# Position bias added to the scores from three bf16 parts, adapters in pairs, and q and k spread in four pieces, in a four-layer transformer kernel

## The chip, the cores and the metric

The kernel runs as one program on one core of a Trainium2 chip. The metric is the device time in microseconds (us) of one execution. The kernel before was timed in three runs; its median is 2657.45 us, between 2647.17 and 2663.92.

## The reference, cut to what matters

x holds rows of D = 128; the kernel works on them in 8 batches of T = 512. Every layer does the same: `xn = layernorm(x)`, then `x = x + attention(xn) + feed_forward(xn)`.

```python
# layers 0 and 2: 16 heads of 8, causal; layer 2 masks with w*mask - (1-mask)*1e6
p = softmax(scores - max); oc = einsum('bhqk,bhkd->bhqd', p, v); return oc @ Wo.T + bo
# layer 0 ffn: 16 experts, top 4 by logits; layer 1 ffn: 8 experts, top 1
# layer 1 attention: 8 heads of 64, linear attention with a decay
S = g4 * S + einsum('bhi,bhj->bhij', kt, vt); z = g3 * z + kt      # q, k = elu + 1
y = num / den * gate
# layer 2 ffn: 8 autoencoders with 32 hidden; the best one's adapter is added
h = relu(einsum('btd,edh->ebth', x, Wd1) + bd1); recon = einsum('ebth,ehd->ebtd', h, Wd2) + bd2
idx = argmin(mean((recon - x) ** 2)); return base + adapter[idx](x)
# layer 3 attention: full, with a position bias of each head
rel = clip(pos[:, None] - pos[None, :] + (N - 1), 0, bias_table.shape[0] - 1)
energy = energy + bias_table[rel].transpose(2, 0, 1)
att = softmax(energy / (sqrt(C) * clip(temperature[0], 0.1, 10.0)))
# layer 3 ffn: top 2 experts chosen by the first token, mean of both
```

## The kernel before, in words

The four layers follow each other; within a layer all work is cut into 8 batches of 512 tokens. Layer 0 and layer 1 end with a routed stretch (the experts, some 485 to 795 us and 1245 to 1385 us of the span). A program of its own for each engine (PE is TensorE, DVE is VectorE, ACT is ScalarE, POOL is GpSimd, SP issues most DMAs) takes steps in the order of one list. `lay_out` (L774) makes it: each step has a time written by hand, in slots, and the list is sorted by it. A step carries the name of what it does; `own(n)` of each layer gives the steps of batch n that aren't attention. So moving a number moves the step past all others on its engine. An engine that waits in one step holds up all that stand behind it.

**Attention, layers 0, 2 and 3.** The 16 heads go in 4 groups of 4 (`HG`, `NG`). q and k are split into three bf16 parts, stored to DRAM (L494, L497) and read back spread over the partitions, so that one matmul of 72 rows (`KROWS`) gives the float32 product. `sp_expand` (L487) does this on SP: two halves of 8 heads, each one DMA for K (L516) and one for Q (L518); each load has a semaphore. The dictionary `behind_row` says which half waits until how many of the previous batch's rows of maxima are in: `{1: 3}` in layers 0 and 2 (half 1 waits for three rows), `{0: 2}` in layer 3 (half 0 waits for two). For each group: `pe_max` (L541, with the mask L547) makes the scores in rows of q, DVE reduces them to maxima (L558, in layer 3 also L564 with the tilted bias `L.tilt`), TensorE turns the maxima (L590), ACT copies them (L597), and `store_max_rows` (L524) sends them with a 12 KB DMA from ACT's queue into the last rows of Q, so that the next product already has the maximum taken off. Then `pe_scores` (L611) makes the scores in columns of k, ACT takes the exponential (L633), TensorE multiplies with v (L648), and the result is turned and divided (L656, L662, L668, L669). The first score of a group waits for that group's stored row. Layers 0 and 2 have 10 score slots a group, 40 a batch; layer 3 has 16, 64 a batch. The turned attention goes through L677 (TensorE) and L682 (ACT), and the output sum is added by DVE (L2217 in layer 2, L2512 in layer 3).

**Bias in layer 3.** `rel` is clipped, so the bias differs from a constant of the head only where the key comes well after the query: in key block kb = 2 for the first 128 queries and in kb = 3 for the first 256 (`far`). `pe_scores` adds it there with a float32 matmul of the identity by `L.bias` (L615, 128 columns; L618, 256 columns). A float32 matmul is two instructions. The table is prepared at the end of layer 2: DVE makes 384 values for each head, `sp_lead` (L2308) stores them (24 KB) and reads them back as a Hankel array (L2313, 2 MB). Sixteen `bias` rounds on TensorE mirror it (L2416, eight) and turn it (L2421, eight), and DVE copies each (L2486).

**Layer 2's rebuilds.** Per batch eight `rebuild` steps (L2157): expert e's hidden part sits on 32 partitions of `L.hd`, and one float32 matmul of 512 columns, two instructions, makes the reconstruction; `differ` on DVE (L2198) subtracts, `square` on ACT (L2128) sums the squares. All eight pass through bank 0, whose ring (`early`) also holds norm, q, k, v and the hidden parts. The ring `late` (bank 1) holds the turned maxima and attention, its projection and the output. `take` on TensorE waits until the reader of the bank's previous user is done, in the ring's fixed order.

**Layer 1.** 48 slots a batch; TensorE L1736, L1750, L1781 and L1789, phi (elu + 1) on POOL L1596 behind ACT L1644 and L1647.

## Time and profile before

| | |
|---|---|
| median of three runs | 2657.45 us |
| profiled execution | 2658.72 us |
| its span | 2656.9 us |
| mean granted TensorE clock | 0.942 |
| busy: TensorE, its weight loads | 2307.9 us (87%), 1430.4 us |
| busy: DVE, ACT, POOL | 1556.5, 1332.5, 566.8 us |
| DMA packets, bytes | 132516, 214.11 MB |

The profile is of one execution, taken by the hardware profiler. The span is the time between its first and last instruction; the execution's time is 1.8 us longer. Busy shares are averages over layers with different limits, so a change has to be read in its own stretch. PE is TensorE's matmuls and PEld its weight loads, which overlap them. The granted clock is given as a share of full speed. ACTq and SPq are the DMA issues of ACT and SP.

### The profile page before, as it was taken

Reading aid. Unit: us, or ns where it says so; the run is one execution under the profiler, and the core shown is the slowest. Engines: PE = TensorE matmul, PEld = TensorE weight load, DVE = VectorE, ACT = ScalarE, POOL = GpSimd, SP = SyncE. Lnnn points to the kernel's source line nnn. Section 1 sums busy time; section 2 is a strip of 40 time slices with the busy share of each in tenths; the row PEclk is TensorE's granted clock in tenths of the full one; section 3 lists DMA queues with packets and bytes.
Section 4 is the critical chain, followed back from the end, with each engine's and each line's share of the span. In section 5 each row is a group of like instructions: output and inputs, shape, how many; then the busy total and the mean of one; then the engine's idle time right before and its main releaser. Section 6 shows DMA issues by size and latency. Waiting matters only on the chain. (4 is left out here: it accounts for less than half of the span.)

```text
span 2656.9 us, 45118 instructions
## 1 busy us (share of the span) xinstructions
PE 2307.9 (87%) x15319; PEld 1430.4 (54%) x15442; DVE 1556.5 (59%) x4327; ACT 1332.5 (50%) x2458; POOL 566.8 (21%) x591
## 2 busy tenths in 40 slices
PE   4898888999985798898977898988898989889986
PEld 2555554799982576677972444444453443344433
DVE  4777777111113677775334766666567777777762
ACT  3555555554544344341342545555554666666665
POOL 2333443000006566650011111111001100011100
PEclk9999999999996899999995989999998999999998
DMA  4222222577771001002651111111121101111101
GB/s 147 70 85 83 71 84 86 172 228 225 230 205 56 26 25 30 28 14 80 192 146 53 53 54 54 54 54 54 55 80 57 35 28 50 55 55 53 39 25 33
DMA packets 132516, 214.11 MB, mean 81 GB/s; under 512 B 22680, under 2 KB 91968, under 8 KB 125376
## 3 DMA queue, kind: packets, MB, share of 16 engines
q1 hardware_dynamic: 120080, 188.79, 23.6%
q0 software_dynamic: 10240, 20.99, 2.5%
q8 instruction: 125, 2.05, 0.3%
q10 hardware_dynamic: 1968, 1.44, 0.2%
q14 instruction: 103, 0.84, 0.1%
HBM read 158.57 MB, written 51.40 MB: 79 GB/s over the span
## 5 line engine op out<-in xcount | busy, mean ns | idle before, releaser
L558 DVE TENSOR_REDUCE arena<-bank 128x1 f32<-128x512 f32 (+4 forms) x1216 | 723.7, 615 | 406.6 <-PE bank L547 248.7
L633 ACT ACTIVATE arena<-bank 128x512 f32<-128x512 f32 x640 | 374.3, 599 | 385.7 <-PE bank L623 380.9
L541 PE MATMUL bank<-arena 125*128 125x512 bf16 (+3 forms) x1536 | 471.6, 345 | 26.7 <-DVE arena L558 11.0
L633 ACT ACTIVATE arena<-bank,inverse_scale 128x512 f32<-128x512 f32 x512 | 336.7, 688 | 197.1 <-PE bank L611 73.0
L611 PE MATMUL bank<-arena 128*128 128x512 bf16 (+3 forms) x1413 | 404.9, 331 | 29.1 <-DMA arena<-arena 17.6
L611 PEld LDWEIGHTS bank<-arena 128*128 128x128 bf16 x1536 | 140.1, 100 | 352.8 <-ACT arena L633 191.9
L648 PE MATMUL bank<-arena 128*32 128x512 f32 (+3 forms) x3072 | 325.6, 508 | 0.9 <-ACT arena L633 0.8
L962 POOL DMA_INDIRECT back_rows<-sorted_out,back_now x160 | 155.9, 974 | 496.6 <-PE bank L623 232.1
L541 PEld LDWEIGHTS bank<-arena 125*128 125x128 bf16 x1536 | 146.1, 101 | 197.1 <-DVE arena L558 86.2
L623 PE MATMUL bank<-mask_k,identb 128*128 128x256 bf16 (+1 forms) x640 | 165.1, 258 | 48.1 <-DMA arena<-arena 45.6
L1243 ACT ACTIVATE arena<-bank,arena 128x256 f32<-128x256 f32 x320 | 131.8, 470 | 144.6 <-PE bank L1293 144.6
L1066 PE MATMUL bank<-arena 128*128 128x128 f32 x1664 | 202.5, 275 | 0.4 <-ACT arena L1243 0.4
L1066 PEld LDWEIGHTS bank<-arena 128*128 128x128 f32 x1664 | 194.0, 192 | 0.7 <-issue 0.6
L1388 DVE TENSOR_TENSOR arena<-bank,arena 128x256 f32<-128x256 f32 x80 | 34.0, 425 | 269.4 <-PE bank L1066 269.4
L547 PE MATMUL bank<-mask_q,identb 128*128 128x128 bf16 (+2 forms) x704 | 181.5, 258 | 0.0
L1189 POOL DMA_INDIRECT sorted_in<-xn,arena x128 | 125.3, 979 | 220.1 <-PE bank L623 162.9
L1293 PE MATMUL bank<-arena 128*128 128x256 f32 x640 | 153.3, 383 | 1.3 <-DMA arena<-in_L_ffn_w 1.1
L648 PEld LDWEIGHTS bank<-arena 128*32 128x32 f32 x3072 | 71.1, 110 | 127.0 <-issue 71.7
L1293 PEld LDWEIGHTS bank<-arena 128*128 128x128 f32 x640 | 116.3, 192 | 15.6 <-DMA arena<-in_L_ffn_w 2.3
L407 POOL TENSOR_SCALAR rstd<-mean_var 128x4 f32<-128x4 f32 x32 | 7.6, 236 | 534.5 <-DVE mean_var L379 502.0
L2157 PE MATMUL bank<-arena 32*128 32x512 f32 x128 | 84.4, 743 | 20.8 <-DVE arena L2198 17.6
L1596 POOL TENSOR_TENSOR arena<-arena 128x512 f32<-128x512 f32 x64 | 81.9, 1280 | 59.4 <-ACT arena L1647 58.0
(264 smaller groups left out, 3631.0 us busy)
## 6 DMA issues: line engine op xcount, KB each, us to landing
arena<-k_parts SPq DMA_DIRECT2D x48, 576.0 KB
arena<-q_parts SPq DMA_DIRECT2D x48, 576.0 KB
arena<-in_L_ffn_w SPq DMA_DIRECT2D x80, 320.0 KB, 3.6
arena<-in_L_ffn_w SPq DMA_DIRECT2D x80, 258.0 KB, 2.9
arena<-sorted_in SPq DMA_DIRECT2D x104, 128.0 KB, 2.8
sorted_out<-arena SPq DMA_DIRECT2D x104, 128.0 KB, 3.5
arena<-in_L_ffn_w SPq DMA_DIRECT2D x24, 512.0 KB, 3.8
k_parts<-arena SPq DMA_DIRECT2D x24, 384.0 KB
```

The source lines that it names most:

```text
L541: ins = pe.matmul(mx[:, k * w:(k + 1) * w], Qx[0:KMAX, h, q * P:(q + 1) * P], Kx[0:KMAX, h, 0:w], start=(k == 0 or not L.causal), stop=not ...
L547: ins = pe.matmul(edge, identb[:], mask_q[:].unsqueeze(1).to_broadcast([P, n_heads, P]), start=False, stop=True, skip_group_check=True)
L558: ins = dve.reduce_max(L.mx[:, g % 2, q, heads[0]:heads[-1] + 1], mx[:, 0:w * len(heads) - far].rearrange("p (j k) -> p j k", k=w - far), ...
L611: ins = pe.matmul(st[:, c:c + w], Kx[:, h, kb * P:(kb + 1) * P], Qx[:, h, T - w:T], start=(c == 0), stop=not (L.causal or far), skip_group ...
L623: ins = pe.matmul(edge, identb[:], mask_k[:].unsqueeze(1).to_broadcast([P, len(at), P]), start=False, stop=True, skip_group_check=True)
L633: act.activation(L.probs[:, n % L.PR, 0:w], st[:, 0:w], ACT.Exp, scale=L.scale).then_inc(L.st_free.sem, 1)
L648: ins = pe.matmul(bank[2][j * VW:(j + 1) * VW, T - w:T], copy_of(L.Vx, b)[:, kb, g * HG + j, :], L.probs[:, (n + i) % L.PR, c:c + w], star ...
L962: pool.indirect_dma_start(back_rows[:, t, k, :], None, L.ys, bass.IndirectOffsetOnAxis(L.back_now[b.parity][:, r:r + 1], 0)).then_inc(L.go ...
L1066: ins = pe.matmul(bank[2 + j % 2][:, h * D:(h + 1) * D], L.hT[j % 2][:, f, h * P:(h + 1) * P], down(j, f), start=(f == 0), stop=(f == 3))
L1189: pool.indirect_dma_start(L.xs, bass.IndirectOffsetOnAxis(L.slot_now[b.parity][:, r:r + 1], 0), xn[b.parity][:, r // TOP0, :], None).then_ ...
L1243: act.activation(L.hT[j % 2][:, c, :], bank[4 + n % 4][:, c % 2 * BLK:(c % 2 + 1) * BLK], ACT.Gelu, bias=L.wbuf[j % 3][:, L.B1 + c:L.B1 + ...
L1293: ins = pe.matmul(bank[4 + n % 4][:, c % 2 * BLK:(c % 2 + 1) * BLK], L.wbuf[j % 3][:, L.W1 + c * P:L.W1 + (c + 1) * P], L.xT[j % 2][:], st ...
```

## The change

Six parts, in one diff.

A. Layer 3: the table is split into three bf16 parts by DVE (four more small operations), stored, and read back by three Hankel loads of 1 MB. The scores' bias is then added straight from them, by three bf16 matmuls with a mirrored identity `flipb` as weights, for either width. The rounds that make `L.tilt` for the maxima are eight instead of sixteen, each of twelve bf16 matmuls of 128 columns.

B. Layer 2: rebuilds 2i and 2i+1 are one step; the even one uses bank 0 and the odd one bank 1. Times of the steps change; in batch 0 the first pair comes before the first maxima, and the loss later.

C. q and k are spread in four pieces of four heads, one semaphore for both loads of a piece; in layers 0 and 2 piece 2 waits for three rows and piece 3 for four, in layer 3 piece 0 for two, piece 2 for three and piece 3 for four.

D. Layer 3: turning, copying and sending of group 1's maxima come 0.8 slots later.

E. Layer 0: the setup that fills the Q and K copies is a step of each of the two copies, so TensorE no longer waits for the second one at the start.

F. Layer 1: phi of batches 0 and 1 is on DVE; the state steps come 2 slots later, `divide`, `weighted` and `turn_y` earlier, `out` 1.4 later.

```diff
-            L.behind_row = {0: 2} if biased else {1: 3}
+            L.rows_late = 0.8 if biased else 0.0
+            L.behind_row = {0: 2, 2: 3, 3: 4} if biased else {2: 3, 3: 4}
...
-            L.kx = [s(f"k_expanded{i}_", 16, 1) for i in range(HALVES)]
-            L.qx = [s(f"q_expanded{i}_", 16, 1) for i in range(HALVES)]
+            L.spread = [s(f"heads_spread{i}_", 32, 1) for i in range(PIECES)]
...
-            for half in range(HALVES):
-                heads = slice(half * H // HALVES, (half + 1) * H // HALVES)
-                if not first and half in L.behind_row:
+            for n, full in enumerate(L.spread):
+                heads = slice(n * HG, (n + 1) * HG)
+                if not first and n in L.behind_row:
                     settle(sp)
-                    sp.wait_ge(L.nmrow.sem, L.nmrow.at(whole(b.index - 1), 16 * L.behind_row[half]))
-                if first and half > 0:
-                    for one in (L.kx[0], L.qx[0]):
-                        settle(sp)
-                        sp.wait_ge(one.sem, one.at(b, 16))
+                    sp.wait_ge(L.nmrow.sem, L.nmrow.at(whole(b.index - 1), 16 * L.behind_row[n]))
+                if first and n > 0:
+                    settle(sp)
+                    sp.wait_ge(L.spread[n - 1].sem, L.spread[n - 1].at(b, 32))
                 sp.dma_start(copy_of(L.Kx, b)[0:KROWS, heads, :], k_rows[:, :, heads, :].rearrange(
-                    "r o h t -> r o (h t)").to_broadcast([NPART * HD, NPART, H * T // HALVES])).then_inc(L.kx[half].sem, 16)
+                    "r o h t -> r o (h t)").to_broadcast([NPART * HD, NPART, HG * T])).then_inc(full.sem, 16)
                 sp.dma_start(copy_of(L.Qx, b)[0:KROWS, heads, :], q_rows[:, :, heads, :].rearrange(
-                    "o r h t -> o r (h t)").to_broadcast([NPART, NPART * HD, H * T // HALVES])).then_inc(L.qx[half].sem, 16)
+                    "o r h t -> o r (h t)").to_broadcast([NPART, NPART * HD, HG * T])).then_inc(full.sem, 16)
...
-                if far and kb == 2:
-                    ins = pe.matmul(st[:, 0:P], ident[:], L.bias[:, h, P:2 * P],
-                                    start=False, stop=True)
-                if far and kb == 3:
-                    ins = pe.matmul(st[:, 0:2 * P], ident[:], L.bias[:, h, 0:2 * P],
-                                    start=False, stop=True)
+                if far:
+                    near = slice(P if kb == 2 else 0, 2 * P)
+                    for n, part in enumerate(L.hankel):
+                        ins = pe.matmul(st[:, 0:(kb - 1) * P], flipb[:], part[:, h, near],
+                                        start=False, stop=(n == NPART - 1))
...
-                    steps += [(begin - LAST_MAX + 3.2, "max_rows", g, 0, b),
-                              (begin - LAST_MAX + 3.8, "copy_rows", g, 0, b),
-                              (begin - LAST_MAX + 4.1, "send_rows", g, 0, b),
+                    turn = begin - LAST_MAX + (L.rows_late if g == 1 else 0.0)
+                    steps += [(turn + 3.2, "max_rows", g, 0, b),
+                              (turn + 3.8, "copy_rows", g, 0, b),
+                              (turn + 4.1, "send_rows", g, 0, b),
...
-                start = [(-41.5, "loaded", 0), (-35.0, "keys", 0), (-20.0, "filled", 0)] if n == 0 else []
+                start = [(-41.5, "loaded", 0), (-35.0, "keys", 0)] if n == 0 else []
+                start += [(-20.0, "filled", n + 1)] if n < L.copies else []
...
-                    steps += [(12.0 * m, "decayed", m), (12.0 * m + 5.0, "fade", m), (3.0 * m - 0.4, "state", m)]
-                    steps += [(weigh + 2.0, "weighted", 2 * m), (weigh + 4.9, "divide", 2 * m),
-                              (weigh + 5.6, "weighted", 2 * m + 1), (weigh + 8.2, "divide", 2 * m + 1)]
-                steps += [(at, "turn_y", c) for c, at in enumerate((34.5, 46.5, UNIT + 8.9, UNIT + 9.9))]
+                    steps += [(12.0 * m, "decayed", m), (12.0 * m + 5.0, "fade", m), (3.0 * m + 1.6, "state", m)]
+                    steps += [(weigh + 2.0, "weighted", 2 * m), (weigh + 4.2, "divide", 2 * m),
+                              (weigh + 4.6, "weighted", 2 * m + 1), (weigh + 6.6, "divide", 2 * m + 1)]
+                steps += [(at, "turn_y", c) for c, at in enumerate((34.5, 46.5, UNIT + 7.6, UNIT + 8.6))]
                 steps += [(-20.5 + 2.0 * c, "turn_k", c) for c in range(CHUNKS)]
-                steps.append((UNIT + 12.2, "out", 0))
+                steps.append((UNIT + 13.6, "out", 0))
...
+                    if b.index < 2:
+                        return
...
-                    step for e in range(E2) for at in [-17.0 + 2.2 * (e - 4) if n == 0 and e > 3 else -31.0 + 1.6 * e]
-                    for step in ((at, "rebuild", e), (at + 0.7, "differ", e), (at + 1.6, "square", e))] + [
-                    (-8.2 if n == 0 else -15.2, "loss", 0), (-7.4 if n == 0 else -14.4, "choose", 0),
+                    step for i in range(E2 // 2) for at in [-17.0 + 4.0 * (i - 1) if n == 0 and i else (-31.8, -28.4, -22.0, -18.4)[i]]
+                    for step in ((at, "rebuild", i), (at + 0.7, "differ", 2 * i), (at + 1.6, "square", 2 * i),
+                                 (at + 0.8, "differ", 2 * i + 1), (at + 2.3, "square", 2 * i + 1))] + [
+                    (-4.5 if n == 0 else -15.2, "loss", 0), (-3.7 if n == 0 else -14.4, "choose", 0),
...
-                def rebuild(pe, L, b, e):
-                    bk = take(pe, L, b, f"r{e}")
-                    rows = slice(HID2 * (e % 4), HID2 * (e % 4 + 1))
-                    fill(L, f"r{e}", pe.matmul(bk[:], L.wd2[rows, e // 4, :], L.hd[rows, e // 4, :],
-                                               start=True, stop=True))
+                def rebuild(pe, L, b, i):
+                    two = (2 * i, 2 * i + 1)
+                    banks = [take(pe, L, b, f"r{e}") for e in two]
+                    for e, bk in zip(two, banks):
+                        rows = slice(HID2 * (e % 4), HID2 * (e % 4 + 1))
+                        fill(L, f"r{e}", pe.matmul(bk[:], L.wd2[rows, e // 4, :], L.hd[rows, e // 4, :],
+                                                   start=True, stop=True))
...
-                sp.wait_ge(L.table_dve, 3)
-                sp.dma_start(L.tabled, L.table[:]).then_inc(L.table_dma, 16)
+                sp.wait_ge(L.table_dve, 7)
+                sp.dma_start(L.tabled, L.table_parts).then_inc(L.table_dma, 16)
                 sp.wait_ge(L.table_dma, 16)
 
-                sp.dma_start(L.hankel[:], bass.AP(L.tabled.tensor, 0, [[1, P], [384, H], [1, HANKEL]])
-                             ).then_inc(L.table_dma, 16)
+                for n, part in enumerate(L.hankel):
+                    sp.dma_start(part, bass.AP(L.tabled.tensor, 384 * n, [[1, P], [384 * NPART, H], [1, HANKEL]])
+                                 ).then_inc(L.table_dma, 16)
                 sp_expand(sp, L, START, True)
...
-                    if n < H // 2:
-                        ins = pe.matmul(bk[:], flip[:], L.hankel[:, 2 * n:2 * n + 2, :].rearrange("p h i -> p (h i)"),
-                                        start=True, stop=True)
-                    else:
-                        for c in range(4):
-                            h, block = 2 * (n - H // 2) + c // 2, slice(P, 2 * P) if c % 2 == 0 else slice(0, P)
-                            ins = pe.transpose(bk[:, c * P:(c + 1) * P], L.bias[:, h, block], ident[:])
+                    for c in range(4):
+                        h, block = 2 * n + c // 2, slice(P, 2 * P) if c % 2 == 0 else slice(0, P)
+                        for i, part in enumerate(L.hankel):
+                            ins = pe.matmul(bk[:, c * P:(c + 1) * P], part[:, h, block], flipb[:],
+                                            start=(i == 0), stop=(i == NPART - 1))
...
+                    dve.tensor_copy(L.table_parts[:, 0, :], L.table[:]).then_inc(L.table_dve, 1)
+                    dve.wait_ge(L.table_dve, 4)
+                    dve.tensor_tensor(L.rest[:], L.table[:], L.table_parts[:, 0, :], ALU.subtract).then_inc(L.table_dve, 1)
+                    dve.wait_ge(L.table_dve, 5)
+                    dve.tensor_copy(L.table_parts[:, 1, :], L.rest[:]).then_inc(L.table_dve, 1)
+                    dve.wait_ge(L.table_dve, 6)
+                    dve.tensor_tensor(L.table_parts[:, 2, :], L.rest[:], L.table_parts[:, 1, :],
+                                      ALU.subtract).then_inc(L.table_dve, 1)
```

## Rows read from the trace of the kernel before

**Rows 1.** Busy time by stretch: us, busy (xinstructions) of each engine, PEclk, DMA share, GB/s

```profile
865.00:1245.00 380.00, 331.47 (x2231) 251.99 (x2230) 274.29 (x825) 135.14 (x238) 203.07 (x194) 0.95 0.09 26
1577.00:1645.00 68.00, 61.09 (x436) 30.94 (x439) 44.97 (x107) 36.22 (x71) 9.98 (x10) 0.95 0.17 53
2188.00:2267.00 79.00, 69.95 (x395) 32.38 (x402) 57.97 (x181) 51.76 (x81) 7.33 (x9) 1.00 0.16 47
```

**Rows 2.** Chain of waits of a layer 3 batch: start us, us, what

```profile
2192.88 0.43 PE bank L618 x2
...
2204.19 0.22 PE bank L541
...
2206.18 6.31 DMA arena<-arena
2213.58 1.00 PE bank L648 x8
```

**Rows 3.** Waits from 2110 to 2580 us: engine, line, waited for, total, times, longest

```profile
PE bank L611 <- DMA arena<-arena: 15.3, 6, 2.9
...
PE bank L590 <- DVE x L2512: 9.7, 6, 1.6
```

**Rows 4.** Timeline where TensorE resumes, layers 0, 2 and 3; brackets: idle before, releaser

```profile
263.22 0.22 PE L623 MATMUL bank<-mask_k,identb 128*128 128x128 bf16 x1 [2.86 <-DMA arena<-arena]
...
1644.18 0.22 PE L623 MATMUL bank<-mask_k,identb 128*128 128x128 bf16 x1 [2.22 <-DMA arena<-arena]
...
2212.54 0.39 PE L611 MATMUL bank<-arena 128*128 128x512 bf16 x1 [2.48 <-DMA arena<-arena]
```

**Rows 5.** Groups by form, 2110 to 2580 us: busy, mean ns, idle before

```profile
L633 ACT ACTIVATE arena<-bank,inverse_scale 128x512 f32<-128x512 f32 x384 | 252.7, 688 | 149.4 <-PE bank L611 57.8 <-PE bank L615 46.7 <-PE bank L618 36.3
```

**Rows 6.** Timeline of layer 2: four 128-column matmuls, then the next

```profile
1593.87 0.39 PE L541 MATMUL bank<-arena 125*128 125x128 bf16 x4
...
1594.10 0.38 PE L547 MATMUL bank<-mask_q,identb 128*128 128x512 bf16 x1
```

**Rows 7.** DMA view from 1953 to 1968 us: issues with KB and us to landing

```profile
q1 hardware_dynamic: 2921, 2.85, 60.3%
...
arena<-bias_by_distance SPq DMA_DIRECT2D x1, 2048.0 KB, 9.1
...
bias_by_distance<-arena SPq DMA_DIRECT2D x1, 24.0 KB, 1.8
```

**Rows 8.** Rebuilds in the chain and timeline of layer 2, row groups in layer 1

```profile
943.03 1.16 PE L1750 MATMUL bank<-arena 64*128 64x128 f32 x16
...
1604.38 1.12 PE bank L2157 x2
...
1616.52 1.42 PE L2157 MATMUL bank<-arena 32*128 32x512 f32 x2 [1.57 <-DVE arena L2198]
```

**Rows 9.** SP's issue of the halves, and the last stretch of the load's tail

```profile
2198.30 0.79 SPq L516 DMA_DIRECT2D arena<-k_parts  x1
...
2218.00:2222.00 4.00, 3.06 (x14) 1.92 (x14) 1.85 (x5) 2.03 (x3) 0.00 (x0) 1.00 0.20 80
```

**Rows 10.** Waits of scores on the stored rows: 123 to 428 us, then 1528 to 1950

```profile
PE bank L623 <- DMA arena<-arena: 20.8, 12, 3.4
...
PE bank L623 <- DMA arena<-arena: 15.5, 9, 2.9
```

**Rows 11.** Four us behind such a stall in layer 0 (columns as in rows 1)

```profile
156.00:160.00 4.00, 3.77 (x20) 1.54 (x22) 2.46 (x10) 1.45 (x3) 0.95 (x1) 0.57 0.09 32
```

**Rows 12.** Timeline of the first batch's start

```profile
27.95 0.83 SPq L516 DMA_DIRECT2D arena<-k_parts  x1
...
43.69 0.59 PE L541 MATMUL bank<-arena 125*128 125x128 bf16 x4 [5.10 <-ACT arena L764]
```

**Rows 13.** Waits in layer 1, 865 to 1245 us

```profile
PE bank L1736 <- issue: 10.3, 7, 1.9
...
PE bank L1789 <- DVE arena L1947: 9.9, 8, 1.8
```

84 lines of the change are left out of this document (48 added, 36 removed).

## The prediction

> **What bounds the kernel now.** I read the busy table by stage first [rows 1]: in one 79 us stretch of layer 3 (a batch is 78.5 us) TensorE is busy for 69.95 us, DVE for 57.97, ACT for 51.76; in layer 2 it is 61.09 of 68 us. So TensorE sets the pace, and two things can give time: fewer or cheaper matmuls, and the 7 to 9 us in which it stands. Then the chain of waits of that batch [rows 2]. It holds the two-pass float32 bias matmuls (0.43 us a pair at 256 columns) and one 6.31 us DMA: the store of group 2's max rows, which ACT's queue issues and which the scores of that group wait for. The table of waits [rows 3] sums this: 15.3 us in six waits, and 9.7 us in six waits of the transposes of L590 for DVE's output sum L2512. The chain starts the store at 2206.18, and in the timeline TensorE starts again at 2212.54 after 2.48 us idle [rows 2, 4].
>
> **A, bias in three bf16 parts (layer 3).** By the code each head has one 128-column (L615) and one 256-column (L618) float32 matmul a batch. The second costs 0.43 [rows 2], the first half of it, 0.22. A bf16 matmul of 512 columns takes 0.22 in the same chain, so 0.055 per 128; and four 128-column ones, each with its own weight load, start within 0.23 us (1593.87 to 1594.10) [rows 6], so loads don't slow them. Three parts then cost 0.165 instead of 0.22, and 0.33 instead of 0.43: 0.155 saved per head, 2.5 a batch, 20 in eight. ACT needs 0.688 us per slot [rows 5]. The slots with bias cost TensorE 0.9 to 1.1 (0.22 max, 0.22 scores, the bias, and a quarter of the 1.00 of L648 [rows 2]), so there it is TensorE that leads and the saving counts; the slots without bias ran at ACT's pace already and won't catch up. I take -18, ends 0 (weight loads exposed after all: six of them at 0.05 a head would give 0.3 back) and -20.
>
> The table behind it moves at the border of layers 2 and 3. One 2 MB load of 9.1 us [rows 7] becomes three of 1 MB, half the bytes a piece of 512 B in place of 1024, three times the pieces. In those 15 us queue q1 moved 2921 packets in 60.3% of sixteen engines' time, 0.050 us each. If one of 512 B costs half, 6144 of them take 6144 x 0.025 / 16 = 9.5 us; if the same, 19. I take the middle, 14: 5 us later than 9.1, and four small DVE operations more. Against it TensorE's sixteen rounds become eight (eight of 0.86 and eight of 0.44, 10.4 us, become eight of twelve bf16 matmuls of 0.055, 5.3) and the sixteen DVE copies eight. I take 0, ends -6 and +12; it is paid once.
>
> **B, rebuilds in pairs (layer 2).** A rebuild is two passes of 512 columns over 32 rows and takes 1.12 us on the chain [rows 8], eight a batch. In pairs two experts sit on different row groups. Layer 1 shows that row groups run side by side: sixteen 64-row passes of 128 columns take 1.16 us, where sixteen at a quarter of the 0.43 that is four such passes would be 1.72 [rows 2, 8]. For 32-row groups I take a pair at the price of one, 1.1 instead of 2.2: 4.4 a batch, 35 in all. Against it each pair now needs bank 1 as well as bank 0. Take pair 0: bank 1 is free only after ACT's copy of the turned attention (L682), an operation of ACT's that I put at 1 us with its turn. Pair 1 waits for the output sum on DVE, some 0.4. TensorE takes its banks in order, and behind the waiting pair stand max, scores and attend of the running group, so nothing covers it. Net 4.4 - 1.4 = 3.0 a batch, -25; ends 0 and -35. The Trainium skill (TensorEngine Tiling (Array Packing), Key Properties) says that changing the tiling mode drains TensorE; four changes in place of eight would be a gain besides, and no row here separates it.
>
> **C, q and k in four pieces.** Four DMAs for the two halves follow each other from 2198.30 on, and the store of the rows at 2206.18. In 2218 to 2222 the DMA share is still 0.20 [rows 9], about 3 of 16 engines: the tail of the q load. The nearest transfer with nothing beside it, a 24 KB store, took 1.8 us [rows 7]; the 12 KB store here took 6.31 [rows 2]. So the wait comes from the bytes in front. With pieces 0 and 1 behind row 2, and 2 behind row 3, half the bytes are in front in layer 3, and the store lands some 2.2 us earlier, between 0 and 4.5. That takes 1.9 of 2.5 us: -13 in seven batches, ends 0 and -18. In layers 0 and 2 half 1 stood in front of group 3's store; now piece 2 does, with half the bytes, and it has 6 to 8 us to pass. Here the whole stall goes: 2.86 us each in layer 0, 2.22 in layer 2 [rows 4]; the tables give 20.8 in layer 0 over five batches and 15.5 in layer 2 over six [rows 10]. Seven batches each: -18 and -13, ends 0 and -29, 0 and -18. What is late next is ACT's exp, which had caught up during the stall, so some of it comes back (in the sum).
>
> After these stalls the granted clock falls: 0.57 in 156 to 160 us [rows 11], and layer 2 shows the same behind its stalls, the 1.2 GHz level for most of it, and TensorE had been idle for 2 to 3 us just before. Four us at 0.57 lose 1.7. In seven batches of each of layers 0 and 2 that could be 24; as the clock falls in other places too and not after each stall, I take -10, ends 0 and -24. SP also issues 8 DMAs of 0.75 us instead of 4 a batch; SP has nothing else that is due.
>
> The Trainium skill (DMA: Bandwidth & Descriptors, Why a DMA increments its semaphore by 16 and not by 1) has the queue take the largest number up to 16 that divides both slowest dimensions: 3 for the q load, in halves or quarters. The 0.20 agrees. That speaks against the change, since pieces don't spread the load; the second rival prices that case from rows.
>
> At the start of layer 0 the first half is issued at 27.95 and TensorE begins at 43.69 after 5.10 idle [rows 12]. The first quarter has half the bytes, and E lets TensorE start without ACT's setup of copy 1. I take -5, ends 0 and -5.1. In layer 2 the first batch's piece 0 lands earlier too and one pair stands before the first max: -4, ends 0 and -5.
>
> **D, rows of group 1 later (layer 3).** The wait on L2512 is 1.6 us a batch [rows 3]; 0.8 slots of 78.5/64 = 1.23 us are 1.0. -5 in all, ends +3 and -10.
>
> **F, layer 1.** TensorE is busy 331.5 of 380 us [rows 1]; waits in what the new order moves are L1789 on DVE 9.9 and L1736 on issue 10.3 [rows 13]. Sixteen phi operations go from POOL to DVE, which has 274.3 of 380 busy; even at ACT's 0.69 for 512 elements [rows 5] they cost 11 there. Two thirds of 20: -13, ends -22 and +6.
>
> **Sum.** Layer 0: -5 -18 -5 (half the clock) = -28. Layer 1: -13. Layer 2: -25 -13 -4 -5 = -47. Border 0. Layer 3: -18 -13 -5 = -36. Together -124. Some 15% of it will turn into waits on ACT and DVE, which have only 20 to 27 us a batch to spare: -18 back, so -106. The profiled execution took 2658.72 (span 2656.9, 1.8 around it), 1.3 above the median of 2657.45; from 2658.7 this gives 2552, and I leave the 1.3 in the range.
>
> **Rivals.**
> *More comes through.* All of the -124 and the clock's other half: 2658.7 - 124 - 14 = 2521. For it: TensorE is the bound nearly everywhere. Against it: ACT's 0.688 per slot. Chance 0.15.
> *The stores are not relieved.* Smaller pieces keep the same engines busy for the same bytes, and if a store waits for the first piece to drain and not by bytes in front, the 44 us of stalls stay and the clock's 10 with them: 54, of which 15% was discounted, so 2552 + 46 = 2598. For it: the share is still 0.20 in 2218 to 2222 [rows 9], when the store has long landed, so bytes in front and bytes behind aren't told apart. Against it: in layers 0 and 2 the piece in front has 6 to 8 us to pass and half the bytes. Chance 0.23, of which 0.05 lies above 2631, where besides the 32-row groups don't overlap.
> *Bank 1 chains layer 2 to the turns (slower).* Place: the second bank of each pair. If a pair waits for the late ring's readers (the copies of turned attention and rows, the output sum) and these sit behind DVE's reduces, TensorE stands, with all of the group's matmuls behind it. Price: x us for each of 32 pairs. It decides from 106/32 = 3.3 us a pair; at 4.5 the time is 2552 + 144 = 2696. For it: ring order is fixed, so one late reader holds all. Against it: with one bank a rebuild in a busy stretch waited 1.57 us for DVE [rows 8]. Chance 0.05, 0.04 of it slower.
> *As forecast* 0.57, own range 2530 to 2580.
>
> The measurement can tell about 1% from no change, 27 us. Faster by more: 0.57 + 0.15 + 0.18 = 0.90; within: 0.05 + 0.01 = 0.06; slower: 0.04. Below, the range takes the outer ends of matmuls, pairs, layer 1 and clock (-2, -10, -9, -14 and half the discount, -9): 2508, and to be safe 2500. Above, it goes past the second rival, to 2615.
>
> **What would show it.** Waits of L611 and L623 on DMA: gone in layers 0 and 2, some 4 us left in layer 3. Busy TensorE in 79 us of layer 3 near 67.5 of a batch of 74 us. Rebuilds: four pieces of 1.1 us on a chain, not eight. Clock 1.00 after group 3's scores. A batch of layer 2 of 62 us instead of 68. If L611 still waits 2.5 us behind the store, C was wrong; if a pair takes 2.1 us, or waits 2 us for its bank, B was; if L2416 starts over 8 us later behind its loads, the border was.

## The result, and the profile after

The changed kernel takes 2560.16 us (median of 4 runs, 2552.73 to 2566.28), the kernel before 2655.16 (4 runs). The ratio is 0.964, with an interval of 0.9598 to 0.9683: 95 us less, where 105 had been forecast (2552, range 2500 to 2615). The profiled execution took 2552.73 with a span of 2550.9. A second set of runs on another chip, told of below, gave 0.9654 (0.9624 to 0.9685).

I first cut both spans at the output sums, which DVE adds once a batch in each layer. These are lines on a single instruction group: its durations, and its first and last start.

The kernel before:

```profile
L1377 DVE TENSOR_TENSOR x<-bank,x x8: 677/680/692, 133.0 to 483.1; 128x512 f32<-128x512 f32 x8
...
L1954 DVE TENSOR_TENSOR x<-bank,x x8: 691/692/692, 934.5 to 1244.7; 128x512 f32<-128x512 f32 x8
...
L2217 DVE TENSOR_TENSOR x<-bank,x x8: 681/682/692, 1541.9 to 1999.6; 128x512 f32<-128x512 f32 x8
...
L2512 DVE TENSOR_TENSOR x<-bank,arena x8: 680/681/691, 2109.9 to 2646.7; 128x512 f32<-128x512 f32 x8
```

The changed kernel (L1379, L1965, L2231 and L2536 are the same four sums):

```profile
L1379 DVE TENSOR_TENSOR x<-bank,x x8: 678/680/691, 123.0 to 451.4; 128x512 f32<-128x512 f32 x8
...
L1965 DVE TENSOR_TENSOR x<-bank,x x8: 691/691/692, 890.8 to 1193.2; 128x512 f32<-128x512 f32 x8
...
L2231 DVE TENSOR_TENSOR x<-bank,x x8: 680/681/691, 1483.6 to 1918.4; 128x512 f32<-128x512 f32 x8
...
L2536 DVE TENSOR_TENSOR x<-bank,arena x8: 680/681/691, 2029.1 to 2541.1; 128x512 f32<-128x512 f32 x8
```

Differences of these starts give the stretches: seven batches of a layer from its first sum to its last, and the starts between. The last column is what the forecast had there before its discount of 18.

| stretch | before | changed | gain | forecast |
|---|---|---|---|---|
| up to layer 0's first sum | 133.0 | 123.0 | 10.0 | 5 |
| layer 0 | 350.1 | 328.4 | 21.7 | 23 |
| to layer 1's first sum | 451.4 | 439.4 | 12.0 | (part of 13) |
| layer 1 | 310.2 | 302.4 | 7.8 | (part of 13) |
| to layer 2's first sum | 297.2 | 290.4 | 6.8 | 4 |
| layer 2 | 457.7 | 434.8 | 22.9 | 43 |
| border of layers 2 and 3 | 110.3 | 110.7 | -0.4 | 0 |
| layer 3 | 536.8 | 512.0 | 24.8 | 36 |

The two profiled spans differ by 106.0 us. That it is just the forecast sum is chance: layers 2 and 3 fell short by 31 us, the starts and layer 1 gave 13 more than was put on them, and the difference happens to be the discount of 18. One stretch differs between executions too: layer 2 of the changed kernel took 434.8 us in this profile and 443.2 in the second one, and in three traces whose layer 2 is that of the kernel before it took 457.7, 459.7 and 464.0. So a few us of a single stretch say nothing, and below I use them only beside waits or beside the timed ratio.

What became of the waits of TensorE for the stored rows and for q ([rows 3] and [rows 10] before), in the changed kernel's tables of waits of layer 0 (123 to 452 us), layer 2 (1484 to 1919) and layer 3 (2029 to 2541):

```profile
PE bank L620 <- DMA arena<-arena: 3.1, 5, 0.9
...
PE bank L620 <- DMA arena<-arena: 9.2, 7, 2.2
...
PE bank L539 <- DMA arena<-q_parts: 7.9, 6, 2.1
...
PE bank L2171 <- ACT arena L679: 7.0, 5, 1.4
...
PE bank L2171 <- DVE x L2231: 5.7, 6, 1.0
...
PE bank L588 <- DVE arena L2212: 5.5, 6, 0.9
...
PE bank L609 <- DMA arena<-arena: 13.4, 6, 2.9
...
PE bank L588 <- DVE x L2536: 4.8, 7, 0.8
```

(L539, L588, L609, L620 and L2171 are L541, L590, L611, L623 and L2157 of before; L679 copies the turned attention, L2212 is `differ`.) In layer 0 the stall is all but gone (20.8 us before, 3.1 after). In layer 2 the 15.5 us of [rows 10] became 9.2 on the stores and 7.9 of a new kind, on the first quarter of q. In layer 3 most of the stall is left: 13.4 us where it was 15.3. The waits of L2171, and that of L588 on L2212, are for bank 1, which the pairs now use too. In exchange, a wait of the kernel before is gone, that of its single rebuilds for DVE's reader of bank 0 (from its table of waits of 1541.9 to 1999.6 us):

```profile
PE bank L2157 <- DVE arena L2198: 10.5, 12, 1.6
```

Busy time of layers 2 and 3, from first sum to last (the columns of [rows 1]), before:

```profile
1541.90:1999.60 457.70, 410.13 (x2907) 210.17 (x2931) 290.44 (x678) 237.28 (x458) 54.09 (x55) 0.94 0.19 59
2109.90:2646.70 536.80, 475.01 (x2656) 218.75 (x2706) 364.04 (x1137) 349.30 (x541) 42.10 (x53) 0.99 0.14 42
```

and after:

```profile
1483.50:1918.30 434.80, 363.88 (x2958) 198.79 (x2981) 286.63 (x674) 235.62 (x456) 54.12 (x55) 0.98 0.20 63
2029.10:2541.10 512.00, 454.76 (x2868) 191.89 (x2921) 361.79 (x1137) 346.70 (x541) 42.15 (x53) 1.00 0.14 44
```

TensorE lost 46 us of busy time in layer 2, but the layer lost only 23 us. In layer 3 it lost 20 busy, which is the term of the bias matmuls. Some of TensorE's records are missing in both of these traces (2656 and 2868 in layer 3, where other traces of the same matmuls have 2706 and 2921); between two complete traces of layer 3, of the run with part F alone and of the second one of the changed kernel, it is 480.6 against 463.8, so 17 us.

### The profile page after: what moved, and what is told of

The parts are those of the page before. It is cut to its first block and busy times, and to the rows that moved or that the text cites. A ratio compares the mean times of both kernels' runs of the same rounds, so it can differ in the third digit from the quotient of the medians.

```text
span 2550.9 us, 45929 instructions
## 1 busy us (share of the span) xinstructions
PE 2208.6 (87%) x15619; PEld 1376.2 (54%) x15746; DVE 1564.6 (61%) x4339; ACT 1327.7 (52%) x2459; POOL 549.0 (22%) x575
## 3 DMA queue, kind: packets, MB, share of 16 engines
q10 hardware_dynamic: 1968, 1.44, 0.2%
## 5 line engine op out<-in xcount | busy, mean ns | idle before, releaser
L630 ACT ACTIVATE arena<-bank 128x512 f32<-128x512 f32 x640 | 372.2, 598 | 324.7 <-PE bank L620 314.0
L539 PE MATMUL bank<-arena 125*128 125x512 bf16 (+3 forms) x1536 | 465.0, 341 | 41.5 <-DVE arena L556 16.8
L609 PE MATMUL bank<-arena 128*128 128x512 bf16 (+3 forms) x1409 | 396.0, 326 | 24.9 <-DMA arena<-arena 13.4
L609 PEld LDWEIGHTS bank<-arena 128*128 128x128 bf16 x1536 | 139.4, 99 | 299.8 <-ACT arena L630 178.8
L539 PEld LDWEIGHTS bank<-arena 125*128 125x128 bf16 x1536 | 143.6, 100 | 197.0 <-DVE arena L556 94.1
L620 PE MATMUL bank<-mask_k,identb 128*128 128x256 bf16 (+1 forms) x640 | 162.3, 254 | 19.8 <-DMA arena<-arena 16.3
L1295 PE MATMUL bank<-arena 128*128 128x256 f32 x640 | 152.0, 381 | 0.6 <-ACT arena L1083 0.3
L1649 ACT ACTIVATE arena<-bank 128x512 f32<-128x512 f32 x64 | 38.1, 595 | 113.1 <-PE bank L1712 113.1
L1809 PE MATMUL bank<-arena 128*128 128x256 f32 x384 | 89.4, 388 | 2.0 <-DMA arena<-in_L_ffn_w 2.0
## 6 DMA issues: line engine op xcount, KB each, us to landing
arena<-in_L_ffn_w SPq DMA_DIRECT2D x24, 512.0 KB, 3.9
```

Of the source, the lines that this page charges most:

```text
L539: ins = pe.matmul(mx[:, k * w:(k + 1) * w], Qx[0:KMAX, h, q * P:(q + 1) * P], Kx[0:KMAX, h, 0:w], start=(k == 0 or not L.causal), stop=not ...
L609: ins = pe.matmul(st[:, c:c + w], Kx[:, h, kb * P:(kb + 1) * P], Qx[:, h, T - w:T], start=(c == 0), stop=not (L.causal or far), skip_group ...
L620: ins = pe.matmul(edge, identb[:], mask_k[:].unsqueeze(1).to_broadcast([P, len(at), P]), start=False, stop=True, skip_group_check=True)
L630: act.activation(L.probs[:, n % L.PR, 0:w], st[:, 0:w], ACT.Exp, scale=L.scale).then_inc(L.st_free.sem, 1)
L1295: ins = pe.matmul(bank[4 + n % 4][:, c % 2 * BLK:(c % 2 + 1) * BLK], L.wbuf[j % 3][:, L.W1 + c * P:L.W1 + (c + 1) * P], L.xT[j % 2][:], st ...
```

## The experiments

Parts are named as in the change, A to F; the edit of a run with a part alone or undone is that part of its diff, shown here where it is short. Each kernel was timed against the kernel before on its own chip.

### One part alone on the kernel before

Part A, the bias:

> The kernel before with part A alone (bias in three bf16 parts, table rounds halved). Theory (matmuls): the saving is TensorE time in the slots with bias; from one output sum to the last of layer 3 (2109.9 to 2646.7, 536.8 us before) some 17 to 20 us go, the border of layers 2 and 3 moves by less than 3, and layers 0 to 2 stay: 2636 to 2640 against 2655. Rival (weight loads or ACT): the slots with bias run at ACT's pace already or the six more weight loads show, and layer 3 loses less than 8 us: 2647 or more.

Measured: ratio 0.9976 (0.9956 to 0.9996), that is 6 us, between 1 and 12 by the interval, and so the rival's size. Layer 3 took 535.2 us, where the two runs of the same chip without A and C (parts B and F alone) have 539.8 and 538.1. The view by stretch of layer 3 of this kernel, and its wait for the stored rows:

```profile
2114.20:2649.40 535.20, 472.03 (x2926) 195.97 (x2926) 362.69 (x1136) 347.64 (x541) 42.07 (x53) 0.97 0.14 42
```

```profile
PE bank L612 <- DMA arena<-arena: 19.8, 6, 3.6
```

It is not the rival's reason of the weight loads: they took less time (196 us, 219 before), not more. The waits for ACT's exponential (L612 on L633) are 5.7 us where they were 5.0, so ACT isn't it either. The wait for the stored row rose from 15.3 to 19.8, as one expects if the store's landing hangs on the load and not on TensorE's work: who comes sooner waits longer. And the granted clock was 0.97, not 0.99. Two hundredths of 475 busy us are 9.5. Why the clock was lower in this profile, the runs don't tell.

Part B, the pairs:

> The kernel before with part B alone (rebuilds in pairs). Theory: the whole gain of layer 2 in the changed kernel (457.7 us between the first and the last output sum became 434.8) is the pairs', since the stalls on loads only moved there: 22 to 26 us shorter in layer 2, 2629 to 2634. Rival (bank 1): the pairs give back most of their 4.4 us a batch in waits for bank 1, and the pieces brought the rest: 5 to 12 us shorter, 2643 to 2650.

Measured: ratio 1.0005 (0.9985 to 1.0024), nothing. Layer 2 became longer, 469.2 us, and its start shorter (290.7 instead of 297.2). Layer 2's stretch, the wait, and one instance with the issue of the first half:

```profile
1529.70:1998.90 469.20, 378.87 (x2937) 203.88 (x2933) 290.01 (x678) 236.67 (x456) 53.86 (x55) 0.93 0.20 58
```

```profile
PE bank L541 <- issue: 45.6, 6, 8.5
```

```profile
1610.20 0.79 SPq L518 DMA_DIRECT2D arena<-q_parts  x1
...
1625.77 0.58 PE L541 MATMUL bank<-arena 125*128 125x128 bf16 x4 [7.47 <-issue]
```

The pairs do save matmul time (378.9 busy instead of 410.1), but the first maxima of the next batch come sooner and find their half of q and k on its way: 7.6 us of waiting in each of six batches, more than the pairs save. Behind the wait shown, the granted clock was 0.50 from 1622 to 1630 us. A wait on a semaphore that is put down to "issue" is one whose releaser the profile does not name; the issue at 1610.20 is the load in question, by the code, in which L541 waits there for both loads of the first half. Both theories were wrong.

Part C, the pieces:

```diff
-            L.behind_row = {0: 2} if biased else {1: 3}
+            L.behind_row = {0: 2, 2: 3, 3: 4} if biased else {2: 3, 3: 4}
...
-            for half in range(HALVES):
-                heads = slice(half * H // HALVES, (half + 1) * H // HALVES)
+            for n, full in enumerate(L.spread):
+                heads = slice(n * HG, (n + 1) * HG)
```

> The kernel before with part C alone (q and k in four pieces, with the new waits behind rows). Theory (a store is late whenever the tail of a q load runs on its three engines, however many bytes are in front): layer 0 gains 20 to 25 us with its start, because the tail ends before the store is issued; layer 2 changes by less than 5 and layer 3 by less than 4, because three and two pieces go out at once there. 2625 to 2633. Rival (the wait follows the bytes in front, as forecast): layer 2 gains 13 and layer 3 13 besides: 2600 to 2608.

Measured: ratio 0.98 (0.9767 to 0.9834), 2610.57 us, 53 us less by the ratio, between the theory and its rival. Layer 0 took 330.0 us, layer 2 430.5, layer 3 530.6 (the profiled execution is the fastest of the four, 10 us under their median). So about half of the whole change or a little more is this part. In this profile it is worth more in layer 2 (27 us) than all parts together; but in the run with part B undone, where layer 2 has C without the pairs too, layer 2 took 442.1 us, so its worth there is between 16 and 27:

```profile
1518.50:1949.00 430.50, 392.36 (x2941) 202.76 (x2933) 289.81 (x678) 237.71 (x459) 53.70 (x55) 0.99 0.19 62
```

With the stall gone the granted clock is 0.99 instead of 0.94, and the same matmuls are busy for 392 us instead of 410. That is 18 us from the clock besides the stall. My theory for this run had layer 2 wrong: with rebuilds one by one, the store of group 3 is issued late enough that the three pieces are all but through (1.6 us of packets left behind the store of 1608.23, 0.7 behind that of 1673.45). In layer 3 the waits for the stored row fell from 15.3 to 10.2 us.

Part F, layer 1:

> The kernel before with part F alone (layer 1: phi of two batches on DVE, steps moved). Theory: the start of layer 1 gains most (from the last output sum of layer 0 to the first of layer 1, 451.4 us before, some 12 us less), the later batches 7 to 8: 2633 to 2637. Rival: the shorter start comes from layer 0's end or from the routed stretch and not from F, and only 7 to 8 are F's: 2647.

Measured: ratio 0.9963 (0.9942 to 0.9985), 10 us, as the rival had it (the theory had 20 to 24), though not for its reason. The start of layer 1 took 446.8 us, and 455.1, 454.6 and 456.3 in the three other kernels of the same chip, which don't have F; layer 1 took 306.1, and 308.8, 305.9 and 308.7 in them. So the start is F's, some 8 us; the later batches gain next to nothing by it. The start of layer 2 took 301.9 us here, where the kernels without F and with single rebuilds have 297.2 to 297.6: F gives some 4 us back there.

The four ratios multiply to 0.9745. The changed kernel is at 0.9654 with interval down to 0.9624, so about 1% is from D, E and from the parts together, give or take half of that by the intervals. E was not tried alone. A hint of it lies in the starts of layer 0: in the four later runs without C and E the first sum stands at 130.2 to 130.8 us (133.0 in the first profile), with C alone at 126.3, and with all parts or all but one between 121.1 and 124.7. So some 4 us are C's and 2 to 5 may be E's.

### One part undone

> The changed kernel with part A undone (float32 bias matmuls, sixteen rounds). Alone on the kernel before, A took 1.6 us off layer 3; the changed kernel as a whole took 24.8 off it. Theory 1 (A pays only when the rows of group 1 and the pieces leave room): layer 3 goes from 512.0 back to 528 to 533 us, ratio to before 0.970 to 0.972. Theory 2 (A is worth nothing anywhere, part D carries the gain): layer 3 stays within 4 us of 512, ratio 0.964 to 0.966.

Measured: 0.9688 (0.9659 to 0.9716), some 9 us over 0.9654 with intervals that still overlap, and layer 3 in 524.1 us at a granted clock of 1.00, with 472.16 us busy:

```profile
2040.00:2564.10 524.10, 472.16 (x2654) 216.25 (x2702) 363.71 (x1136) 349.16 (x542) 42.05 (x53) 1.00 0.14 43
```

Against 512.0 and 515.4 in the two profiles of the changed kernel, and 517.2 with part B undone, A is worth 7 to 12 us in layer 3. That lies between the two theories. TensorE's busy time moves by 17 to 20 at the same clock, so about half of the matmul saving came through. Where some of the rest went, the waits for the stored row tell: 11.0 us here and 13.4 with A, as they are 15.3 without and 19.8 with it on the kernel before.

```diff
-            L.rows_late = 0.8 if biased else 0.0
+            L.rows_late = 0.0
```

> The changed kernel with part D undone (rows of group 1 not 0.8 slots later). Theory 1 (D is worth its wait on the output sum): the wait of L588 on L2536 goes from 4.8 to 10 us and layer 3 is 5 us longer. Theory 2 (D carries what A alone does not show): layer 3 is 12 to 18 us longer, ratio 0.969 to 0.971. Rival to both (late rows only shift the store into the pieces): layer 3 is shorter by 1 to 3 us.

Measured: 0.9664 (0.962 to 0.9708), which can't be told from 0.9654. Layer 3 took 521.3 us, and the wait of L588 on L2536 rose from 4.8 to 11.1 us, by some 6 us, as theory 1 had it.

> The changed kernel with part B undone (eight rebuilds one by one). Theory (with pairs, layer 2 is bound by when the first quarter of q and k is in, so the matmul time saved turns into waits): layer 2 goes from 434.8 to 429 to 432 us, and the stretch between the last output sum of layer 1 and the first of layer 2 from 290.5 back to 297; in total nothing, ratio 0.964 to 0.967, and TensorE has 25 to 30 us more of busy time in layer 2. Rival (pairs pay once the pieces are there, as forecast): layer 2 rises by 20 us or more, ratio 0.972.

Measured: 0.9683 (0.9648 to 0.9718), some 8 us over 0.9654 and not clear of the noise. Layer 2 took 442.1 us with 395.7 busy, beside 434.8 and 443.2 with 363.9 busy in the first of these; the start of layer 2 took 302.4 instead of 290.4 and 286.4. Thirty-two us less of busy TensorE bring layer 2 some 3 us or nothing, and its start some 12, of which 4 or 5 only make good what F costs there without pairs. The ratio and layer 2 lie outside what the theory gave (it had layer 2 shorter without pairs), but the rival's 20 us are excluded, and the theory's reason stands: matmul time turned into waits. The two tables of waits say which. Here TensorE waits 13.3 us for the readers of bank 0 in its single rebuilds, 3.8 for stored rows and not at all for q. In the changed kernel it waits 14.8 in the pairs (7.0 and 5.7 above, and 2.1 on L666), 5.5 in L588 on L2212, 5.8 in the loss L2177 for the last square, 9.2 for stored rows and 7.9 for q: 43 us against 17.

### Other waits before the pieces

The timeline of layer 3 in the changed kernel (SP's issues are pieces, ACT's is group 2's store):

```profile
2114.38 0.80 SPq L516 DMA_DIRECT2D arena<-k_parts  x1
...
2115.22 0.73 SPq L518 DMA_DIRECT2D arena<-q_parts  x1
...
2115.99 0.78 SPq L516 DMA_DIRECT2D arena<-k_parts  x1
...
2116.81 0.71 SPq L518 DMA_DIRECT2D arena<-q_parts  x1
...
2120.64 0.75 ACTq L524 DMA_DIRECT2D arena<-arena  x1
...
2127.12 0.77 SPq L516 DMA_DIRECT2D arena<-k_parts  x1
...
2127.15 0.39 PE L609 MATMUL bank<-arena 128*128 128x512 bf16 x1 [2.94 <-DMA arena<-arena]
```

SP's piece 2 waits for that very row, so its issue at 2127.12 tells when the store was in: 6.5 us after its own issue. This batch is the worst of six; in the others it is 5.4 to 6.1, the median of all 5.6, where it was 6.31 with two halves in front ([rows 2]). With no load beside it, it is 2.2 us (a store at 2145.60, and the piece behind it at 2147.80). In layer 2 three pieces go out one behind the other, since the third row, stored from 1491.35 on, is in before SP is through with pieces 0 and 1; both the first maxima and the store wait:

```profile
1492.51 0.81 SPq L516 DMA_DIRECT2D arena<-k_parts  x1
...
1496.64 0.72 SPq L518 DMA_DIRECT2D arena<-q_parts  x1
...
1502.15 0.40 PE L539 MATMUL bank<-arena 125*128 125x128 bf16 x4 [1.85 <-DMA arena<-q_parts]
...
1506.92 0.73 ACTq L524 DMA_DIRECT2D arena<-arena  x1
...
1512.33 0.78 SPq L516 DMA_DIRECT2D arena<-k_parts  x1
```

```diff
-            L.behind_row = {0: 2, 2: 3, 3: 4} if biased else {2: 3, 3: 4}
+            L.behind_row = {0: 2, 1: 3, 3: 4} if biased else {2: 3, 3: 4} if n == 0 else {2: 4}
...
-                if first and n > 0:
+                if (first or L.n == 2) and n == 1 or first and n > 1:
```

> The changed kernel with other waits before the pieces: in layer 2 piece 1 waits for piece 0 to be in and pieces 2 and 3 for the fourth row; in layer 3 piece 1 waits for the third row. Theory (a store is about 4 us late whenever the tail of a q load is on its three engines, and the first quarter is late when two others load beside it): the waits on stores and on q_parts in layer 2 (17 us) go nearly all, and the waits of L609 on stores in layer 3 (13.4) go to under 4; 18 to 28 us less than the changed kernel, ratio to before 0.954 to 0.958. Rival (the stores' delay is their own, whatever loads): waits of L609 and L620 stay at 13 and 9, ratio 0.961 or more.

Measured: 2545.28 us, ratio 0.9561 (0.9532 to 0.959), clear of the changed kernel's. Layer 3 took 499.5 us, and its table of waits has no wait of a matmul on a stored row left (of the weight loads, 3.8 us). The same store:

```profile
2114.38 0.80 SPq L516 DMA_DIRECT2D arena<-k_parts  x1
...
2120.34 0.75 ACTq L524 DMA_DIRECT2D arena<-arena  x1
...
2123.15 0.77 SPq L516 DMA_DIRECT2D arena<-k_parts  x1
```

With one piece in front, of which 2.0 us were left at the issue, it is in after 2.8 us; with two and 7.1 us left, after 6.5. Layer 3's half of the theory holds. Layer 2 stayed at 438.2 us, though its waits on loads fell from 17.1 to 4.3 us. Others grew in their place: the loss L2177 for the last square on ACT from 5.8 to 12.0, and a single wait in the last batch (L2182 on L666) from 4.4 to 8.5. Behind the first the clock fell:

```profile
PE bank L2177 <- ACT arena L2140: 12.0, 6, 2.6
...
PE bank L539 <- DMA arena<-q_parts: 2.5, 3, 1.2
...
PE bank L620 <- DMA arena<-arena: 1.8, 3, 0.9
```

```profile
1632.00:1636.00 4.00, 2.55 (x16) 1.68 (x20) 2.40 (x5) 2.52 (x7) 0.15 (x1) 0.64 0.25 77
```

Next came the changed kernel itself once more, this version with a later loss, and one with a single number changed on the kernel before (`{1: 3}` to `{1: 4}`). The expectations call the version just told of order_both, and the next two late_loss and late_half.

> The changed kernel itself, on the chip of the other runs of this call, so that they can be compared with it directly. Ratio to before 0.960 to 0.968, and layer 2 between 432 and 440 us, layer 3 between 510 and 517.

Measured: 2565.78 us, 0.9654 (0.9624 to 0.9685); layer 2 443.2 us, above the 440 expected, layer 3 515.4.

```diff
-                    (-4.5 if n == 0 else -15.2, "loss", 0), (-3.7 if n == 0 else -14.4, "choose", 0),
+                    (-4.5 if n == 0 else -13.6, "loss", 0), (-3.7 if n == 0 else -12.8, "choose", 0),
```

> The kernel with the other waits before the pieces (as in order_both), and besides layer 2's loss and choice 1.6 slots later from the second batch on. With the loads in time, TensorE stood 2 to 2.6 us a batch in L2177 for the last squares on ACT (12.0 us in six batches), and the granted clock fell behind it (0.64). Theory (that wait took the place of the ones on loads): layer 2 goes from 438.2 to 420 to 427 us, 2528 to 2535 in all, ratio to before 0.950 to 0.953. Rival (ACT and DVE bound layer 2 and another wait follows at once): layer 2 stays within 4 us of 438, ratio 0.956.

Measured: 2541.32 us, 0.955 (0.9523 to 0.9577): 24 us under the changed kernel on the same chip, but no better than order_both. Layer 2 434.9. The wait of L2177 is gone, and 8.8 us of waits on stores (L609) and 7.2 of L588 on L2212 stand where 1.8 (L620) and 5.4 stood. The rival holds here.

```diff
-            L.behind_row = {0: 2} if biased else {1: 3}
+            L.behind_row = {0: 2} if biased else {1: 4}
```

> The kernel before with one number changed: in layers 0 and 2 half 1 of q and k waits for four rows instead of three. Theory (what part C brought is that no load's tail is out when group 3's store is issued, and quarters aren't needed for it): layer 0 goes from 350 to 328 to 332 us and layer 2 from 458 to 430 to 436, layer 3 stays; 2610 to 2618, ratio 0.980 to 0.984. Rival (the smaller pieces themselves matter): the half comes too late or delays the next row, and the gain is under half of that, ratio 0.990 or more.

Measured: 2644.63 us, 0.9941 (0.9919 to 0.9962): 16 us, a third of what C brings, as the rival had it. Layer 0 took 338.9 us and layer 2 442.0, about half of the gain in each; the profiled execution is 10 us under the median. The stall of group 3 goes, but the half is too long for the gap to the next batch's first store:

```profile
201.68 0.78 SPq L516 DMA_DIRECT2D arena<-k_parts  x1
...
209.78 0.73 ACTq L524 DMA_DIRECT2D arena<-arena  x1
...
216.36 0.39 PE L611 MATMUL bank<-arena 128*128 128x512 bf16 x1 [2.62 <-DMA arena<-arena]
```

So the waits alone don't do it. That the short pieces alone don't either, layer 3 of the changed kernel shows, where most of the stall stayed; for layers 0 and 2 no run tried it. As far as was tried, both are needed: pieces short enough to fit between two stores, and waits that put them there.

Last, the pairs were moved away from the sums and turns that share bank 1 (and the loss and choice to -12.4 and -11.6):

```diff
-                    step for i in range(E2 // 2) for at in [-17.0 + 4.0 * (i - 1) if n == 0 and i else (-31.8, -28.4, -22.0, -18.4)[i]]
+                    step for i in range(E2 // 2) for at in [-17.0 + 4.0 * (i - 1) if n == 0 and i else (-31.8, -28.4 if n == 0 else -24.4, -20.8, -17.4)[i]]
```

> late_loss with layer 2's pairs at other times from the second batch on: pair 1 at -24.4 instead of -28.4, behind the turn of the maxima and not right behind the output sum, pairs 2 and 3 at -20.8 and -17.4, loss and choice at -12.4 and -11.6. Theory (what the pairs lose is waits for bank 1): the waits of L2171 on the output sum (5.7 us) and of L588 on L2212 (7.2) go, layer 2 goes from 434.9 to 420 to 427 us, ratio to before 0.950 to 0.953. Rival (layer 2 is at what ACT and DVE give out in this order, and each wait taken away returns elsewhere): those waits go and layer 2 stays within 4 us of 435, ratio 0.955.

Measured: 2526.5 us, 0.9504 (0.9485 to 0.9523), the fastest of all, with layer 2 in 426.1 us:

```profile
1478.00:1904.10 426.10, 363.73 (x2985) 198.38 (x2981) 284.11 (x674) 233.56 (x456) 53.76 (x55) 0.98 0.21 65
```

```profile
PE bank L659 <- DVE arena L2212: 9.8, 6, 1.6
...
PE bank L588 <- DVE arena L2212: 4.6, 5, 1.1
...
PE bank L609 <- DMA arena<-arena: 4.5, 10, 1.0
```

The wait of the pairs on the output sum is gone, those of L588 and L609 are smaller, and a new one on bank 1 (L659, 9.8) came. By its numbers the theory holds, at the edge of its range; by its reason only in part, since a wait for bank 1 came back elsewhere, as the rival had it. Busy TensorE is as in late_loss (365.5), so the 9 us are waits alone; as one kernel's layer 2 differs by 8 us between profiles, the ratio (0.955 before, intervals that just touch) is the better evidence for a gain. Against the changed kernel, the two ratios to before stand at 0.9504 and 0.9654.

## Why the prediction was right, and where its steps failed

The sign, the size and the reason at large were right: TensorE sets the pace, and stalls behind row stores plus matmul time were to be had. By its steps:

- **Layer 0, stall and start: right.** 21.7 us for the seven batches where 18 and half the clock's 10 were put; the start gave 10 instead of 5, of which 2 or 3 lie in this one profile of the kernel before (133.0, and 130.2 to 130.8 in four other kernels with the same start). How the rest divides between C and E was not tried.
- **C in layer 3, "half the bytes are in front ... the store lands some 2.2 us earlier": wrong.** It landed 5.6 us after its issue (median of six; 6.31 in [rows 2]), some 0.7 us earlier and not 2.2, and the wait fell from 15.3 to 13.4 us, not by 13 (to 10.2 with C alone; A brings TensorE to it sooner). By the prediction's own sign, a wait of L611 of 2.5 us, C was wrong here: it is 2.2 us in the mean and 2.9 at most. The step took the delay as proportional to the bytes in front. It is not, as long as the load has more than some 4 us to run; the last section has the numbers. The second rival was nearer for this layer. Letting the tail end within some 2 us of the issue gave 12 to 16 us (499.5 against 512.0 and 515.4).
- **C in layer 2, "here the whole stall goes": right with C alone, wrong in the company of B.** With C alone 1.1 us of waits on stores are left of 16.0. I had taken that piece 2 alone is in front; with pairs all three are, and the first quarter is late too.
- **The clock, -5 in layer 2: far too small.** With the stalls gone it rose from 0.94 to 0.99, and 18 us of busy time went with C alone. In the two profiles of the changed kernel it was 0.98 and 0.95.
- **B, "net -25": this step failed most.** A pair takes 1.13 us as forecast, and 32 us of busy time went. In layer 2 next to nothing came of it. I had priced the waits for bank 1 at 1.4 us a batch; there were 2.1 a batch on L679 and the sum (12.7 in six), and 0.9 more on the turn of the maxima. But the waits for the readers of bank 0 went, which I hadn't counted: 20.3 us in all for the banks against 13.3 with B undone, so net this was no more than priced. What I had put at nothing is when the first piece of the next batch is due once the batch is shorter (7.9 us for q, and 5.4 more for stored rows than with B undone), and the loss, which now waits for ACT's last square (5.8). Together these take back 26 of the 32 us. The sign "a batch of layer 2 of 62 us instead of 68" was met by number only: it is 62.1, but over seven batches it had been 65.4, not 68. The slower rival named the right place but a price that never came near 3.3 us a pair.
- **A, -18: TensorE's share right, its worth half.** 17 to 20 us less busy, 7 to 12 us less time. The step "there it is TensorE that leads and the saving counts" overlooked that TensorE then waits longer for the stored row, which lands when it lands.
- **D, -5: right** (L588's wait from 10.7 over seven batches to 4.8).
- **F, -13: right in all**, by its start: 10 us alone (between 4 and 15), 20 in the two stretches of layer 1 in the changed kernel.
- **The border: right.** The three Hankel loads were issued from 1878.60 on, and the first bias matmul began at 1891.93, after 13.3 us; 14 had been taken:

```profile
1878.60 1.97 SPq L2331 DMA_DIRECT2D arena<-bias_by_distance  x2
...
1891.93 0.27 PE L2436 MATMUL bank<-flipb,arena 128*128 128x128 bf16 x2 [0.86 <-DMA back_rows<-bias_by_distance]
```

The discount of 15% for waits that come in place of others was the right thought and too small for layers 2 and 3: 79 us had been put on the two, and 48 came, of 66 us of busy time that went. That the total fits all the same is luck in part: what was missing there came in at the starts and in layer 1.

## What to carry to other kernels

Time that is taken from one engine is only worth what the next due date leaves: before pricing a shorter stretch, look up when its loads are issued and when the shorter stretch will ask for them. A small store that others wait for should be issued when no long load's tail is out; here cutting the load into pieces helped much only where each piece was held back so that its tail ended before the store or within some 2 us of it. Run parts alone and undone: here one of six carried about half of the gain, and the one with the largest busy saving carried next to nothing in its own layer.

## What the runs showed of the hardware that I had not expected

A 12 KB store issued on ACT's queue while a load's tail kept about 3 of 16 engines busy (share 0.18 to 0.21 in 2120 to 2126 us of the changed kernel) was in after 5.4 to 6.6 us (1506.92 to 1512.33 in layer 2, 6.31 in [rows 2], 209.78 to 216.36 in late_half), whether the load in front came in pieces of 8 heads or of 4; with 2.0 us of the load left it took 2.8, and with no load 2.2. That the DMA engines as a whole were four fifths idle did not help it. The DMA records show where the time goes. SP's packets are on queue q1, the store's 15 on q10. The changed kernel's store of 2120.64 has none in 2120 to 2124.7 (first line, q1 alone) and all in 2124.7 to 2127.2 (second line); order_both's store of 2120.34 has all in 2121.7 to 2123.2 (third line):

```profile
q1 hardware_dynamic: 90, 0.34, 18.4%
...
q10 hardware_dynamic: 15, 0.01, 1.5%
...
q10 hardware_dynamic: 15, 0.01, 2.4%
```

So the first packet went 4.1 us after the issue there and 1.4 here. The 14 traces hold 1344 such stores; what tells them apart is how long SP's load in front (packets of 4 KB and more) still goes on. With no more than 2.5 us of it left at the issue, the first packet goes after 1.4 us in the median. With 8 us or more left (77 stores) it goes after 3.9 to 5.1 us, however much is left. With 3 to 4 us left it goes about when the load ends, after 3 us in the median. So, as these traces have it, a store starts when the load in front has ended, or some 4 us after its issue, whichever is sooner.

By the Trainium skill (DMA: Bandwidth & Descriptors, Queues, rings and completion order) an engine takes turns between queues packet by packet. The trace agrees once the store has started: its packets of 1 KB then come some 0.2 us apart on an engine, between the load's of 0.16 us each, and take 1.9 us in all where they take 0.2 with no load. The 2.7 us by which the first packet is late that rule does not explain, and no run here shows what does.

The granted clock moved more than the stalls themselves would say: taking 15 us of stalls out of layer 2 raised it from 0.94 (0.92 and 0.93 in two other traces with the same layer 2) to 0.99, and busy TensorE fell from 410 to 392 us with it. In layer 0 it rose from 0.97 or 0.98 to 1.00 in every profile with part C.
